# Who adds the last layer's bias: twelve instructions move from VectorE to GpSimd

## The chip, the cores and the metric

The kernel runs on one core of a Trainium2 chip. Its time is the device time of one launch in microseconds (us); the number given is the median of several runs. Before the change it is 401.47 us (three runs, 401.32 to 401.8). The engines are TensorE (PE: matmuls; PEld: its weight loads), VectorE (DVE), ScalarE (ACT), GpSimd (POOL) and SyncE (SP), which issues the DMAs. Each runs its own list of instructions in order; they wait for each other by semaphores. SBUF is the on-chip memory, PSUM the banks into which TensorE writes.

## The reference

`x` is 64 x 128 x 128 (batch, row, feature), `adj` 128 x 128. Cut to what matters:

```python
h = maximum(layernorm(x), 0)
# layer 0: two graph convolutions, then four LSTMs over windows of p rows (p = 1..4)
h = relu(adj @ (h @ Wg0 + bg0));  h = relu(adj @ (h @ Wg1 + bg1))
for p in 1..4:
    windows of p rows of h -> LSTM p (gates i, f, g, o) -> the last hidden
    state replaces the window's last row of h
x = x + h
# layer 1, "the last layer"
h = maximum(layernorm(x), 0)
h0, h1, h2 = h @ W[0], h @ W[1], h @ W[2]
out = diag(adj) * h0 + triu(adj, 1) @ h1 + tril(adj, -1) @ h2 + bias
x = x + out
```

The bias is a vector of 128 features, the same for every batch and row.

## The kernel before

The 64 batches are worked on in four groups of 16 (`GROUPS`, `G`), numbered 0 to 3. A group's layer 0 is 22 LSTM units, k = 0 to 21, in two streams (halves of 8 batches). While group i is in its units, the last layer of group i-1 is woven into them, piece by piece: so the last layers of groups 0, 1 and 2 lie inside the units of groups 1, 2 and 3, called the second, third and fourth pass here. The last layer of group 3 stands alone at the end of the program. A group's 16 batches are four quads (`PACK` = 4 batches, 128 x 512 elements), q = 0 to 3.

What one quad goes through in the last layer, by line:

- The statistics (L1074, L938 to L950 on VectorE) give the negative mean MINUS2 and a variance; GpSimd makes the inverse root of it, RS2 (L387, in `rstd`, a power). 
- Centring: H3 = relu(X - mean). For quads 0 and 1 ScalarE does it, in `centre_up` (L821, semaphore `turned_up`); for quads 2 and 3 VectorE subtracts in `centre` (L1101, semaphore `centred`).
- The bias: X = X + BIAS, `add_bias` (L1117, 128 x 512). It can't come before the centring has read X.
- TensorE transposes H3 (L596); ScalarE and VectorE split the result into two parts, HTH (L799) and HTL (L1108, `turn_down`).
- TensorE multiplies by the three weight matrices, `last_value` (L607 to L609); ScalarE copies the result out of PSUM with RS2 as scale (L812).
- VectorE adds the diagonal term to X, `add_own` (L1129); TensorE makes the two other terms, `last_side` (L615); VectorE adds them to X, `add_out` (L1138), and SyncE stores the quad.

The places of these steps are written out by hand. `START_MID`, `START_BETWEEN` and `START_LATE` say behind which part of which unit VectorE does a step for which quad (`OWN`, `ADD`, `CENTRE`, `SHIFT`, `LOW`; quad -1 is quad 3 of the group before that). `SHIFT` is the bias. `START_LATE` puts it behind unit 5 for quad 0, behind unit 6 for quads 1 and 2, and behind unit 9 for quad 3. In group 3, whose last layer stands alone, GpSimd already adds the bias for quads 0 and 1 (L441), and VectorE for quads 2 and 3. `on_pool` tells who does it, and the stores and `add_own` wait accordingly.

An LSTM unit on VectorE is a chain: the products of gates (L993 where the unit is a window's first step; L996, L1006, L1014 otherwise), then, when ScalarE has made the tanh (L884), the hidden state (L1048), its rounded part (L1052, a cast) and the rest (L1060). TensorE's later units read the last two.

GpSimd's list per group (`group`, L419 to L429) is: the inverse roots for the next group's first layernorm (RS1), and two for this group's RS2. 

Of the kernel before, what the change touches and what calls it, by code (L numbers as in the profile page):

```python
# [8 lines left out]
ALU = mybir.AluOpType  # L9
ACT = mybir.ActivationFunctionType  # L10

B, T, D = 64, 128, 128
G = 16
GROUPS = B // G
# [48 lines left out]
def last_unit(k, s):  # L63
# [23 lines left out]

FILL = {4: 6, 9: 6}

LOW, OWN, ADD, CENTRE, SHIFT = "low", "own", "add", "centre", "shift"  # L90
LAST = QUADS - 1
ON_SCALAR = QUADS // 2

# [12 lines left out]
START_BETWEEN = {0: ((LOW, 0),), 1: ((ADD, -1),), 14: ((ADD, 2),)}  # L106
START_MID = {0: ((OWN, -1),), 4: ((LOW, 1),), 5: ((ADD, 0),), 7: ((OWN, 1),), 8: ((LOW, 2),),
             9: ((ADD, 1),), 12: ((OWN, 2),), 13: ((LOW, 3),)}
START_LATE = {4: ((OWN, 0),), 5: ((CENTRE, 2), (SHIFT, 0)), 6: ((SHIFT, 1), (SHIFT, 2))}
STEADY = Plan(  # L110
    at={**START, (15, 1): (Piece(VALUE, 12, 0, (TURN, 3)),), (16, 3): (Piece(VALUE, 13, 1, (SUM, 2)),),
        (17, 3): (Piece(VALUE, 14, 0, (FORGET, 16)),), (18, 3): (Piece(VALUE, 15, 1, (FORGET, 17)),)},
    f_after={**START_F, 16: (VALUE, 12), 17: (VALUE, 13), 18: (VALUE, 14), 19: (VALUE, 15)},
    quads=QUADS, between=START_BETWEEN, mid=START_MID, late={**START_LATE, 9: ((CENTRE, 3), (SHIFT, 3))})


LATE = Plan(at=START, f_after={**START_F, 16: (TURN, 3), 17: (SUM, 2)}, quads=LAST,
            between=START_BETWEEN, mid=START_MID, late={**START_LATE, 9: ((CENTRE, 3), (SHIFT, 3))})
PLANS = (None,) + (GROUPS - 2) * (STEADY,) + (LATE,)

def on_pool(g, q):

    return g == GROUPS - 1 and q < ON_SCALAR


def shifts_to(g, q):

    return QUADS * g + q + 1 - (ON_SCALAR if g == GROUPS - 1 else 0)  # L130


def present(g, n):
# [27 lines left out]
def program(nc, x_tbd, adj_t, adj_diag, wg0, bg0_col, wg1, bg1, wih_t, whh_t, bih_t, bhh_t, w_l1, bias, out_tbd):  # L161
    with ExitStack() as ctx:
# [171 lines left out]
        @block.sync  # L334
        def _(sp):

            sp.dma_start(X[:, 0:HALF, :], x_tbd[:, 0:HALF, :]).then_inc(x_first, 16)
            for q in range(QUARTERS):
                part = slice(HALF if q == 0 else q * G // QUARTERS, (q + 1) * G // QUARTERS)
                sp.dma_start(X[:, part, :], x_tbd[:, part, :]).then_inc(x_quarter[q], 16)  # L340
                if q == 0:
                    sp.dma_start(ADJ[:, :], adj_t).then_inc(w_adj, 16)
            sp.dma_start(WG0[:, :], wg0).then_inc(w_gcn, 16)
            sp.dma_start(BG0[:, :], bg0_col).then_inc(w_gcn, 16)
            sp.dma_start(WG1[:, :], wg1).then_inc(w_gcn, 16)
            sp.dma_start(BG1[:, :], bg1.rearrange("(a n) -> a n", a=1).broadcast_to([T, D])).then_inc(w_gcn, 16)
            sp.dma_start(BI[:, :], bih_t).then_inc(w_gcn, 16)
            sp.dma_start(BH[:, :], bhh_t).then_inc(w_gcn, 16)
            sp.dma_start(WI[:, :, :], wih_t).then_inc(w_ih, 16)
            sp.dma_start(WH[:, :, :], whh_t).then_inc(w_hh, 16)  # L350
            sp.dma_start(WL1[:, :, :], w_l1).then_inc(w_late, 16)
            sp.dma_start(DIAG[:, :], adj_diag).then_inc(w_late, 16)
            sp.dma_start(BIAS[:, :], bias.rearrange("(a n) -> a n", a=1).broadcast_to([T, D])).then_inc(w_late, 16)
            for g in range(1, GROUPS):
                sp.dma_start(X[:, g * G:(g + 1) * G, :], x_tbd[:, g * G:(g + 1) * G, :]).then_inc(x_rest, 16)


            def store(i):
                for q in range(QUADS):
                    pieces = END_PIECES if i == GROUPS - 1 and q == LAST else ((0, PACK),)  # L360
                    for n, (lo, hi) in enumerate(pieces):
                        if on_pool(i, q):
                            sp.wait_ge(pool_shifted, q + 1)
                        else:
                            sp.wait_ge(shifted_x, shifts_to(i, q))
                        sp.wait_ge(out_ready, QUADS * i + q + 1 + n)
                        part = slice(i * G + q * PACK + lo, i * G + q * PACK + hi)
                        sp.dma_start(out_tbd[:, part, :], X[:, part, :]).then_inc(stored, 16)

            for i in range(GROUPS):  # L370
                store(i)
            sp.wait_ge(stored, 16 * (GROUPS * QUADS + len(END_PIECES) - 1))


        @block.gpsimd
        def _(pool):
            pool.memset(ONES[:, :], 1.0).then_inc(consts, 1)
            pool.memset(NHALF[:, :], -0.5).then_inc(consts, 1)
            pool.memset(IDENT[:, :], 0.0).then_inc(consts, 1)
            pool.wait_ge(consts, 3)  # L380
            pool.affine_select(out=IDENT[:, :], in_=IDENT[:, :], compare_op=ALU.not_equal, fill=1.0,
                               base=0, pattern=[[-1, 128]], channel_multiplier=1).then_inc(consts, 1)

            def rstd(ve, var, count, rs, done, lo, hi):

                pool.wait_ge(var, count)
                pool.tensor_tensor(rs[:, lo:hi], ve[:, lo:hi], NHALF[:, lo:hi], ALU.pow).then_inc(done, 1)  # L387

            pool.wait_ge(consts, 2)
            for q in range(QUARTERS):  # L390
                part = slice(q * G // QUARTERS, (q + 1) * G // QUARTERS)
                rstd(VE1, var1, 2 * q + 2, RS1, rs1, part.start, part.stop)
                pool.wait_ge(rs1, q + 1)
                pool.tensor_tensor(SHIFT1[:, part], MINUS1[:, part], RS1[:, part], ALU.mult).then_inc(shift1, 1)


            pool.wait_ge(consts, 4)
            pool.wait_ge(w_adj, 16)

            for k, sign in enumerate((1, -1)):  # L400
                pool.affine_select(out=ADJ2[:, k, :], in_=ADJ[:, :], compare_op=ALU.is_gt, fill=0.0,
                                   base=0, pattern=[[-sign, T]], channel_multiplier=sign).then_inc(consts, 1)


            pool.wait_ge(w_ih, 16)
            done = 0
            for p in range(POOL_SKIPS):
                pairs = [(WI[:, p, :], WIH[:, p, :], WIL[:, p, :])]
                if p:
                    pool.wait_ge(w_hh, 16)  # L410
                    pairs.append((WH[:, p - 1, :], WHH[:, p - 1, :], WHL[:, p - 1, :]))
                for w, high, low in pairs:
                    pool.tensor_copy(high, w).then_inc(split_w, 1)
                    done += 1
                    pool.wait_ge(split_w, done)
                    pool.tensor_tensor(low, w, high.bitcast(F32), ALU.subtract).then_inc(split_w, 1)
                    done += 1

            def group(i):  # L419
                if i == 0:  # L420
                    for s in range(STREAMS):
                        rstd(VE1, var1, 2 * (QUARTERS + s + 1), RS1, rs1, HB * s, HB * s + HB)
                else:
                    rstd(VE1, var1, 2 * (QUARTERS + i + 2), RS1, rs1, 0, G)
                for s in range(STREAMS):
                    if i > 0:

                        pool.wait_ge(value_sb, G * (i - 1) + HB * (s + 1))
                    rstd(VE2, var2, 2 * STREAMS * i + 2 * s + 2, RS2, rs2, HB * s, HB * s + HB)  # L429

            for i in range(GROUPS - 1):
                group(i)
            i = GROUPS - 1
            for q in range(QUADS):
                pool.wait_ge(value_sb, G * (i - 1) + PACK * (q + 1))
                rstd(VE2, var2, 2 * STREAMS * i + 2 * q + 2, RS2, rs2, PACK * q, PACK * q + PACK)
                if on_pool(i, q):
                    pool.wait_ge(w_late, 48)
                    pool.wait_ge(centred, ON_SCALAR * i + q + 1)
                    part = slice(i * G + q * PACK, i * G + (q + 1) * PACK)  # L440
                    pool.tensor_tensor(X[:, part, :], X[:, part, :],  # L441
                                       BIAS[:, :].unsqueeze(1).broadcast_to([T, PACK, D]),
                                       ALU.add).then_inc(pool_shifted, 1)


        @block.tensor
# [480 lines left out]
        def _(dve):  # L927
# [183 lines left out]

            def add_bias(g, q):

                if q < ON_SCALAR and g < GROUPS - 1:
                    dve.wait_ge(turned_up, ON_SCALAR * g + q + 1)
                part = slice(g * G + q * PACK, g * G + (q + 1) * PACK)
                dve.tensor_tensor(X[:, part, :], X[:, part, :], BIAS[:, :].unsqueeze(1).broadcast_to([T, PACK, D]),  # L1117
                                  ALU.add).then_inc(shifted_x, 1)
# [1 line left out]
            def add_own(g, q, lo=0, hi=PACK):  # L1120

                dve.wait_ge(value_sb, G * g + q * PACK + hi)
                if on_pool(g, q):
                    dve.wait_ge(pool_shifted, q + 1)
                elif g == GROUPS - 1:
                    dve.wait_ge(shifted_x, shifts_to(g, q))
                part = bass.ds(g * G + q * PACK + lo, hi - lo)
                own = as_batches(values(q)[:, 0, :])[:, lo:hi, :]
                dve.scalar_tensor_tensor(out=X[:, part, :], in0=own, scalar=DIAG[:, 0:1],  # L1129
# [47 lines left out]
            def last_step(what, g, q, plan):  # L1177
# [2 lines left out]
                    return  # L1180
                if what == CENTRE:
                    centre(g, q)
                elif what == SHIFT:
                    add_bias(g, q)
                elif what == LOW:
                    turn_down(g, q, home(plan, TURN, q))
                elif what == OWN:
# [137 lines left out]
```

## Time and profile before

| | |
|---|---|
| median of the timed runs | 401.47 us |
| span of the profiled execution, first to last instruction | 399.1 us |
| what the median has beside that span | 2.4 us |
| TensorE matmuls, busy | 393.3 us (99%) |
| VectorE, busy | 346.5 us (87%) |
| ScalarE, busy | 287.4 us (72%) |
| GpSimd, busy | 44.0 us (11%) |
| granted TensorE clock | full in all 40 slices |

The profile is one execution. "Busy" of TensorE counts modelled ends of matmuls that overlap, so small waits of it are seen better in the starts of successive matmuls than in this number. A line of the timeline gives the start and the duration of an instruction (or of a row of equal ones), and in brackets the time that the engine stood still before it, with what ended that.

### The profile page before, as it was taken

Reading aid. Unit: us, or ns where it says so; the run is one execution under the profiler, and the core shown is the slowest. Engines: PE = TensorE matmul, PEld = TensorE weight load, DVE = VectorE, ACT = ScalarE, POOL = GpSimd, SP = SyncE. Lnnn points to the kernel's source line nnn. Section 1 sums busy time; section 2 is a strip of 40 time slices with the busy share of each in tenths; the row PEclk is TensorE's granted clock in tenths of the full one; section 3 lists DMA queues with packets and bytes.
Section 4 is the critical chain, followed back from the end, with each engine's and each line's share of the span. In section 5 each row is a group of like instructions: output and inputs, shape, how many; then the busy total and the mean of one; then the engine's idle time right before and its main releaser. Section 6 shows DMA issues by size and latency. Waiting matters only on the chain.

```text
span 399.1 us, 6598 instructions
## 1 busy us (share of the span) xinstructions
PE 393.3 (99%) x2394; PEld 345.3 (87%) x2394; DVE 346.5 (87%) x886; ACT 287.4 (72%) x579; POOL 44.0 (11%) x44
## 2 busy tenths in 40 slices
PE   8999999999999999999999999999999999999997
PEld 7787889998987789899877879899797788989886
DVE  6569999998998998887998898988898979787897
ACT  4668777875897777777689676777589677767554
POOL 4910200100300003000110000300020000000250
PEclk9999999999999999999999999999999999999999
DMA  7830000000000000000000000000000000000003
GB/s 205 315 140 2 0 0 2 2 0 2 0 1 2 26 28 0 28 2 1 2 16 10 28 0 29 0 28 1 2 2 26 0 28 26 2 26 3 0 0 133
DMA packets 5503, 11.18 MB, mean 28 GB/s; under 512 B 1120, under 2 KB 2528, under 8 KB 4960
## 3 DMA queue, kind: packets, MB, share of 16 engines
q1 hardware_dynamic: 5472, 10.77, 7.5%
q8 instruction: 19, 0.31, 0.4%
q14 instruction: 12, 0.10, 0.1%
HBM read 6.57 MB, written 4.19 MB: 27 GB/s over the span
## 4 chain that ended last, share of the span: by engine, by line
PE 79%; DVE 14%; ACT 4%; issue 1%; DMA 1%; POOL 0%; SPq 0%; DVEq 0%; ACTq 0%
PE PS L549 11%; PE PS L540 11%; PE PS L541 10%; PE PS L572 6%; PE PS L569 6%; PE PS L568 6%; PE PS L615 5%; PE PS L490 4%; PE PS L480 4%; PE PS L472 4%; PE PS L457 3%; PE PS L607 3%; PE PS L608 3%; PE PS L609 3%; ACT GT L869 2%; PE PS L582 1%
## 5 line engine op out<-in xcount | busy, mean ns | idle before, releaser
L869 ACT ACTIVATE GT<-PS,BG 128x256 f32<-128x256 f32 (+2 forms) x312 | 157.9, 563 | 17.5 <-PE PS L572 12.8
L540 PE MATMUL PS<-HH,WIH 128*128 128x256 f32 (+2 forms) x312 | 107.2, 344 | 0.1
L541 PE MATMUL PS<-HH,WIL 128*128 128x256 f32 (+2 forms) x312 | 102.7, 330 | 0.0
L549 PE MATMUL PS<-HL,WIH 128*128 128x256 f32 (+2 forms) x294 | 97.3, 331 | 0.6
L884 ACT ACTIVATE TC<-CS 128x512 f32<-128x512 f32 (+2 forms) x88 | 44.9, 510 | 43.6 <-DVE CS L1014 32.5
L387 POOL TENSOR_TENSOR RS<-VE,NHALF 128x4 f32<-128x4 f32 (+2 forms) x18 | 29.9, 1661 | 344.5 <-DVE VE L950 263.9
L540 PEld LDWEIGHTS PS<-HH,WIH 128*128 128x128 f32 x312 | 58.8, 188 | 9.3 <-DVE HH L1052 4.3
L541 PEld LDWEIGHTS PS<-HH,WIL 128*128 128x128 f32 x312 | 58.9, 189 | 3.9 <-issue 1.2
L549 PEld LDWEIGHTS PS<-HL,WIH 128*128 128x128 f32 x294 | 55.5, 189 | 6.6 <-DVE HL L1060 2.4
L572 PE MATMUL PS<-SL,WHH 128*128 128x256 f32 (+2 forms) x192 | 60.1, 313 | 0.2
L568 PE MATMUL PS<-SH,WHH 128*128 128x256 f32 (+2 forms) x192 | 59.9, 312 | 0.0
L569 PE MATMUL PS<-SH,WHL 128*128 128x256 f32 (+2 forms) x192 | 59.7, 311 | 0.0
L572 PEld LDWEIGHTS PS<-SL,WHH 128*128 128x128 f32 x192 | 36.3, 189 | 2.1 <-DVE SL L1060 0.9
L568 PEld LDWEIGHTS PS<-SH,WHH 128*128 128x128 f32 x192 | 36.2, 189 | 1.5 <-DVE SH L1052 0.2
L996 DVE TENSOR_TENSOR IC<-GT 128x256 f32<-128x256 f32 (+2 forms) x48 | 23.8, 496 | 15.6 <-ACT GT L869 15.4
L569 PEld LDWEIGHTS PS<-SH,WHL 128*128 128x128 f32 x192 | 36.3, 189 | 1.3
L1048 DVE TENSOR_TENSOR HT<-GT,TC 128x256 f32<-128x256 f32 (+2 forms) x48 | 23.8, 495 | 5.8 <-ACT TC L884 4.8
L993 DVE TENSOR_TENSOR CS<-GT 128x512 f32<-128x512 f32 (+2 forms) x40 | 23.9, 597 | 2.6 <-ACT GT L869 2.3
L1060 DVE TENSOR_TENSOR SL<-HT,SH 128x256 fp32r<-128x256 f32 (+2 forms) x48 | 23.9, 497 | 1.5
L812 ACT ACTIVATE WH<-PS,RS 128x384 f32<-128x384 f32 x32 | 17.7, 578 | 10.2 <-PE PS L609 9.6
L1014 DVE TENSOR_TENSOR CS<-IC,CS 128x256 f32<-128x256 f32 (+3 forms) x48 | 23.4, 488 | 1.6
L1048 DVE TENSOR_TENSOR HF<-GT,TC 128x512 f32<-128x512 f32 (+2 forms) x32 | 18.9, 591 | 6.4 <-ACT TC L884 5.7
(95 smaller groups left out, 655.5 us busy)
## 6 DMA issues: line engine op xcount, KB each, us to landing
out_tbd<-X SPq DMA_DIRECT2D x15, 256.0 KB, 2.0
X<-x_tbd SPq DMA_DIRECT2D x3, 1024.0 KB, 12.9
WI<-wih_t SPq DMA_DIRECT2D x1, 1024.0 KB, 5.2
X<-x_tbd SPq DMA_DIRECT2D x3, 256.0 KB, 3.7
WH<-whh_t SPq DMA_DIRECT2D x1, 768.0 KB, 6.6
X<-x_tbd SPq DMA_DIRECT2D x2, 128.0 KB, 2.4
WL<-w_l SPq DMA_DIRECT2D x1, 192.0 KB, 6.4
WG<-wg SPq DMA_DIRECT2D x2, 64.0 KB, 2.8
```

Of the source, the lines that this page charges most:

```text
L387: pool.tensor_tensor(rs[:, lo:hi], ve[:, lo:hi], NHALF[:, lo:hi], ALU.pow).then_inc(done, 1)
L540: pe.matmul(dst, WIH[:, p - 1, cols], x_high, start=True, stop=False)
L541: pe.matmul(dst, WIL[:, p - 1, cols], x_high, start=False, stop=False)
L549: mm = pe.matmul(dst, WIH[:, p - 1, cols], x_low, start=False, stop=(j == 0))
L568: pe.matmul(dst, WHH[:, p - 2, cols], SH[:, s, 0:n], start=False, stop=False)
L569: pe.matmul(dst, WHL[:, p - 2, cols], SH[:, s, 0:n], start=False, stop=False)
L572: pe.matmul(dst, WHH[:, p - 2, cols], SL[:, s, 0:n], start=False, stop=True).then_inc(gate_mm, 1)
L869: act.activation(GT[:, s, q, 0:n], bank(s, q)[:, 0:n], ACT.Tanh if q == C else ACT.Sigmoid, bias=BG[:, 4 * (p - 1) + q:4 * (p - 1) + q + 1 ...
L884: act.activation(TC[:, s, done:n], CS[:, s, done:n], ACT.Tanh).then_inc(tanh_ready, 1)
L993: dve.tensor_tensor(CS[:, s, 0:n], GT[:, s, I, 0:n], GT[:, s, C, 0:n], ALU.mult).then_inc(cell_ready, 1)
L1048: dve.tensor_tensor(full, o, tc, ALU.mult).then_inc(lstm_step, 1)
L1060: dve.tensor_tensor(low, full, high.bitcast(F32), ALU.subtract).then_inc(h_out, 1)
```

## The change

The bias of groups 0, 1 and 2 is added by GpSimd. VectorE's twelve instructions for it (four a group) and the table entries `SHIFT` go. GpSimd gets twelve, at the end of its `group(i)`: behind the second inverse root of RS2, each with a wait on `turned_up` (quads 0, 1) or `centred` (quads 2, 3). `add_own` and the stores wait for GpSimd's semaphore. Group 3 stays as it was: GpSimd for quads 0 and 1, VectorE for 2 and 3.

```diff
-START_LATE = {4: ((OWN, 0),), 5: ((CENTRE, 2), (SHIFT, 0)), 6: ((SHIFT, 1), (SHIFT, 2))}
+START_LATE = {4: ((OWN, 0),), 5: ((CENTRE, 2),), 9: ((CENTRE, 3),)}
...
 def on_pool(g, q):
 
-    return g == GROUPS - 1 and q < ON_SCALAR
+    return g < GROUPS - 1 or q < ON_SCALAR
...
+def pool_shifts_to(g, q):
+
+    return QUADS * g + q + 1
...
+            def add_bias(g, q):
+
+                part = slice(g * G + q * PACK, g * G + (q + 1) * PACK)
+                pool.tensor_tensor(X[:, part, :], X[:, part, :],
+                                   BIAS[:, :].unsqueeze(1).broadcast_to([T, PACK, D]),
+                                   ALU.add).then_inc(pool_shifted, 1)
+
             def group(i):
...
                     rstd(VE2, var2, 2 * STREAMS * i + 2 * s + 2, RS2, rs2, HB * s, HB * s + HB)
+                pool.wait_ge(w_late, 48)
+                for q in range(QUADS):
+                    if q < ON_SCALAR:
+                        pool.wait_ge(turned_up, ON_SCALAR * i + q + 1)
+                    else:
+                        pool.wait_ge(centred, ON_SCALAR * i + q - ON_SCALAR + 1)
+                    add_bias(i, q)
...
@@ VectorE @@
             def add_bias(g, q):
 
-                if q < ON_SCALAR and g < GROUPS - 1:
-                    dve.wait_ge(turned_up, ON_SCALAR * g + q + 1)
                 part = slice(g * G + q * PACK, g * G + (q + 1) * PACK)
...
                 dve.wait_ge(value_sb, G * g + q * PACK + hi)
                 if on_pool(g, q):
-                    dve.wait_ge(pool_shifted, q + 1)
-                elif g == GROUPS - 1:
-                    dve.wait_ge(shifted_x, shifts_to(g, q))
+                    dve.wait_ge(pool_shifted, pool_shifts_to(g, q))
+                else:
+                    dve.wait_ge(shifted_x, shifts_to(q))
```

GpSimd's list where group 0 ends and group 1 begins. RS1 and RS2 are the inverse roots, X the batches. Before:

```order
L387 TENSOR_TENSOR RS1<-VE1,NHALF 128x8 [waits var1] x2
L387 TENSOR_TENSOR RS2<-VE2,NHALF 128x8 [waits var2] x2
L387 TENSOR_TENSOR RS1<-VE1,NHALF 128x16 [waits var1]
L387 TENSOR_TENSOR RS2<-VE2,NHALF 128x8 [waits var2,value_sb] x2
L387 TENSOR_TENSOR RS1<-VE1,NHALF 128x16 [waits var1]
```

And after (`rstd` is on L392, `add_bias` on L427 there):

```order
L392 TENSOR_TENSOR RS1<-VE1,NHALF 128x8 [waits var1] x2
L392 TENSOR_TENSOR RS2<-VE2,NHALF 128x8 [waits var2] x2
L427 TENSOR_TENSOR X<-X,BIAS 128x512 [waits turned_up,w_late]
L427 TENSOR_TENSOR X<-X,BIAS 128x512 [waits turned_up]
L427 TENSOR_TENSOR X<-X,BIAS 128x512 [waits centred] x2
L392 TENSOR_TENSOR RS1<-VE1,NHALF 128x16 [waits var1]
L392 TENSOR_TENSOR RS2<-VE2,NHALF 128x8 [waits var2,value_sb] x2
```

Four adds stand behind a group's second RS2 and in front of the next group's RS1.

VectorE's list in units 5 to 7 of the second pass. H3 is the centred copy; IC and CS are products of gates. Before:

```order
L1101 TENSOR_TENSOR H3<-X,MINUS2 128x512 [waits var2,x_quarter0]
L1117 TENSOR_TENSOR X<-X,BIAS 128x512 [waits turned_up]
L996 TENSOR_TENSOR IC<-GT 128x512 [waits gate_act]
L1006 TENSOR_TENSOR CS<-GT,CS 128x512 [waits gate_act]
L1014 TENSOR_TENSOR CS<-IC,CS 128x512 [waits lstm_step]
L931 BN_STATS ST1<-X 128x6 x4
L1048 TENSOR_TENSOR HF<-GT,TC 128x64x4x2 [waits tanh_ready]
L1052 CAST HH<-HF 128x64x8 [waits lstm_step]
L1060 TENSOR_TENSOR HL<-HF,HH 128x64x8 [waits lstm_step]
L1117 TENSOR_TENSOR X<-X,BIAS 128x512 [waits turned_up]
L1117 TENSOR_TENSOR X<-X,BIAS 128x512
L996 TENSOR_TENSOR IC<-GT 128x512 [waits gate_act]
```

And after:

```order
L1116 TENSOR_TENSOR H3<-X,MINUS2 128x512 [waits var2,x_quarter0]
L1011 TENSOR_TENSOR IC<-GT 128x512 [waits gate_act]
L1021 TENSOR_TENSOR CS<-GT,CS 128x512 [waits gate_act]
L1029 TENSOR_TENSOR CS<-IC,CS 128x512 [waits lstm_step]
L946 BN_STATS ST1<-X 128x6 x4
L1063 TENSOR_TENSOR HF<-GT,TC 128x64x4x2 [waits tanh_ready]
L1067 CAST HH<-HF 128x64x8 [waits lstm_step]
L1075 TENSOR_TENSOR HL<-HF,HH 128x64x8 [waits lstm_step]
L1011 TENSOR_TENSOR IC<-GT 128x512 [waits gate_act]
```

The three adds are gone, and each time the product IC, which waits for ScalarE's gates, comes next. TensorE's and ScalarE's lists are the same before and after.

## Rows read from the trace of the kernel before

**Rows 1.** Page, busy us (share of the span) and instructions, by engine:
```profile
PE 393.3 (99%) x2394; PEld 345.3 (87%) x2394; DVE 346.5 (87%) x886; ACT 287.4 (72%) x579; POOL 44.0 (11%) x44
```
**Rows 2.** Timeline of VectorE, second pass: start us, us, engine, line, instruction, idle before:
```profile
123.53 0.75 DVE L1129 SCALAR_TENSOR_TENSOR X<-WI,DIAG,X 128x512 f32<-128x512 f32 x1
...
128.18 0.69 DVE L1117 TENSOR_TENSOR X<-X,BIAS 128x512 f32<-128x512 f32 x1
129.90 0.69 DVE L996 TENSOR_TENSOR IC<-GT 128x512 f32<-128x512 f32 x1 [1.04 <-ACT GT L869]
...
134.50 1.29 DVE L1117 TENSOR_TENSOR X<-X,BIAS 128x512 f32<-128x512 f32 x2
135.94 0.69 DVE L996 TENSOR_TENSOR IC<-GT 128x512 f32<-128x512 f32 x1 [0.15 <-ACT GT L869]
...
146.87 0.51 DVE L996 TENSOR_TENSOR IC<-GT 128x336 f32<-128x336 f32 x1 [0.27 <-ACT GT L869]
```
**Rows 3.** Timeline of GpSimd, inverse roots of the second and third pass:
```profile
106.61 1.64 POOL L387 TENSOR_TENSOR RS<-VE,NHALF 128x8 f32<-128x8 f32 x1 [4.22 <-DVE VE L950]
154.42 3.09 POOL L387 TENSOR_TENSOR RS<-VE,NHALF 128x16 f32<-128x16 f32 x1 [46.17 <-DVE VE L950]
...
200.63 1.64 POOL L387 TENSOR_TENSOR RS<-VE,NHALF 128x8 f32<-128x8 f32 x1 [5.93 <-DVE VE L950]
```
**Rows 4.** Timeline of GpSimd, at the start and in the last 25 us:
```profile
5.09 1.02 POOL L387 TENSOR_TENSOR RS<-VE,NHALF 128x4 f32<-128x4 f32 x1 [3.38 <-DVE VE L950]
...
376.02 1.52 POOL L387 TENSOR_TENSOR RS<-VE,NHALF 128x4 f32<-128x4 f32 x1 [78.39 <-ACT WH L812]
377.51 1.27 POOL L441 TENSOR_TENSOR X<-X,BIAS 128x512 f32<-128x512 f32 x1
...
381.18 1.55 POOL L441 TENSOR_TENSOR X<-X,BIAS 128x512 f32<-128x512 f32 x1
```
**Rows 5.** Timeline of VectorE beside these last three:
```profile
375.98 0.69 DVE L1101 TENSOR_TENSOR H<-X,MINUS 128x512 f32<-128x512 f32 x1
...
380.84 0.74 DVE L1129 SCALAR_TENSOR_TENSOR X<-WH,DIAG,X 128x512 f32<-128x512 f32 x1
```
**Rows 6.** Timeline of VectorE beside the inverse root at 154.42:
```profile
155.15 0.51 DVE L1060 TENSOR_TENSOR SL<-HT,SH 128x336 fp32r<-128x336 f32 x1
```
**Rows 7.** GpSimd's smallest sum, one line's instructions: ns min/median/max:
```profile
L394 POOL TENSOR_TENSOR SHIFT<-MINUS,RS x4: 199/199/199, 6.2 to 11.2; 128x4 f32<-128x4 f32 x4
```
**Rows 8.** Timeline of VectorE, second pass, units 0 and 1:
```profile
107.87 0.69 DVE L993 TENSOR_TENSOR CS<-GT 128x512 f32<-128x512 f32 x1 [0.15 <-ACT GT L869]
109.26 0.70 DVE L1048 TENSOR_TENSOR HF<-GT,TC 128x512 f32<-128x512 f32 x1 [0.70 <-ACT TC L884]
109.99 0.43 DVE L1052 CAST HH<-HF 128x512 fp32r<-128x512 f32 x1
110.34 0.68 DVE L1108 SCALAR_TENSOR_TENSOR HTL<-PS,HTH 128x512 fp32r<-128x512 f32 x1
```
**Rows 9.** Timeline of TensorE, second pass, the first product of the last layer:
```profile
111.54 0.34 PE L607 MATMUL PS<-WLH,HTH 128*128 128x384 f32 x1
```
**Rows 10.** Timeline of VectorE, third pass, units 0 and 1:
```profile
202.01 0.69 DVE L993 TENSOR_TENSOR CS<-GT 128x512 f32<-128x512 f32 x1 [0.33 <-ACT GT L869]
202.62 0.74 DVE L1129 SCALAR_TENSOR_TENSOR X<-WH,DIAG,X 128x512 f32<-128x512 f32 x1
203.40 0.69 DVE L1048 TENSOR_TENSOR HF<-GT,TC 128x512 f32<-128x512 f32 x1
...
207.54 0.68 DVE L1138 TENSOR_TENSOR X<-PS,X 128x512 f32<-128x512 f32 x1
```
**Rows 11.** Timeline of TensorE, third pass, the product that waits for L1138:
```profile
208.59 0.34 PE L607 MATMUL PS<-WLH,HTH 128*128 128x384 f32 x1
```
**Rows 12.** Timeline of TensorE, second pass, a short stop:
```profile
140.20 0.32 PE L541 MATMUL PS<-HH,WIL 128*128 128x336 f32 x1
140.67 0.42 PE L549 MATMUL PS<-HL,WIH 128*128 128x336 f32 x1
```

More of the change, by code:

```diff
@@ L88 @@
 FILL = {4: 6, 9: 6}
-LOW, OWN, ADD, CENTRE, SHIFT = "low", "own", "add", "centre", "shift"
+LOW, OWN, ADD, CENTRE = "low", "own", "add", "centre"
 LAST = QUADS - 1
@@ L113, with shifts_to @@
     f_after={**START_F, 16: (VALUE, 12), 17: (VALUE, 13), 18: (VALUE, 14), 19: (VALUE, 15)},
-    quads=QUADS, between=START_BETWEEN, mid=START_MID, late={**START_LATE, 9: ((CENTRE, 3), (SHIFT, 3))})
+    quads=QUADS, between=START_BETWEEN, mid=START_MID, late=START_LATE)
 LATE = Plan(at=START, f_after={**START_F, 16: (TURN, 3), 17: (SUM, 2)}, quads=LAST,
-            between=START_BETWEEN, mid=START_MID, late={**START_LATE, 9: ((CENTRE, 3), (SHIFT, 3))})
+            between=START_BETWEEN, mid=START_MID, late=START_LATE)
 PLANS = (None,) + (GROUPS - 2) * (STEADY,) + (LATE,)
 def on_pool(g, q):
-    return g == GROUPS - 1 and q < ON_SCALAR
-def shifts_to(g, q):
-    return QUADS * g + q + 1 - (ON_SCALAR if g == GROUPS - 1 else 0)
+    return g < GROUPS - 1 or q < ON_SCALAR
+def pool_shifts_to(g, q):
+    return QUADS * g + q + 1
+def shifts_to(q):
+    return q + 1 - ON_SCALAR
 def present(g, n):
@@ L362, in store @@
                         if on_pool(i, q):
-                            sp.wait_ge(pool_shifted, q + 1)
+                            sp.wait_ge(pool_shifted, pool_shifts_to(i, q))
                         else:
-                            sp.wait_ge(shifted_x, shifts_to(i, q))
+                            sp.wait_ge(shifted_x, shifts_to(q))
                         sp.wait_ge(out_ready, QUADS * i + q + 1 + n)
@@ L437, in _ @@
                 if on_pool(i, q):
-                    pool.wait_ge(w_late, 48)
                     pool.wait_ge(centred, ON_SCALAR * i + q + 1)
[L440 to L443, printed above, removed]
+                    add_bias(i, q)
         @block.tensor
@@ L1182, in last_step @@
                     centre(g, q)
-                elif what == SHIFT:
-                    add_bias(g, q)
                 elif what == LOW:
```

## The prediction

> **What bounds the kernel now.** I began with the busy times on the page: TensorE 99%, VectorE 87%, GpSimd 11% [rows 1]. So what matters is not how much VectorE does but whether it makes TensorE stop. The second view was the timeline of VectorE at the bias adds that go. The reader is to see the bracket behind each: after the first add the next instruction, IC on L996, comes after 1.04 us of idleness, after the pair at 134.50 after 0.15 us, and after the add in front of 146.87 after 0.27 us, each time ended by ScalarE's gate (L869), which in turn waits for TensorE [rows 2]. The third and fourth pass show the same instructions with about the same spacing. The third view was GpSimd's timeline, for when the new adds can run [rows 3] and for what happens when both engines are at work [rows 4, 5, 6]. The last was VectorE and TensorE side by side where the new adds will fall [rows 8 to 11].
>
> **What goes.** Four adds a group, twelve in all, at 0.60 to 0.69 us each (a pair takes 1.29) [rows 2]: some 8 us of VectorE's time. Each stood in a gap that ScalarE's gates ended, so VectorE only waits longer: 1.04 + 0.6 us at the first place, 0.15 + 1.2 at the second, 0.27 + 0.6 at the third. Gain: 0. The edits of waits cost nothing: `add_own` for quad 0 comes at 123.53 [rows 2], some 12 us after GpSimd can be done with it (below), and the other quads have more room. The stores wait for `out_ready`, which comes later than the bias in either kernel.
>
> **What comes, and when.** GpSimd's adds stand behind the second RS2 of a group. This ends at 106.61 + 1.64 = 108.25 in the second pass and at 200.63 + 1.64 = 202.27 in the third [rows 3]; the fourth repeats the third. ScalarE's centring is over by then, so the adds for quads 0 and 1 start at once, one after the other. The add for quad 2 follows the centring that ends about where the old add began, 128.2, and ends near 129.5, inside the gap before 129.90 [rows 2]: it meets nothing. The one for quad 3 runs from about 146.0 to 147.2 and meets IC at 146.87 [rows 2], 0.3 to 0.5 us of delay. TensorE has a whole unit of the other stream to do before it reads what comes of this IC, so I cost it at 0; without that cover it would be 3 x 0.45 = 1.4 us. GpSimd's next inverse root comes at 154.42 [rows 3], 7 us later.
>
> How long is such an add? Alone 1.27 us (at 377.51) [rows 4], twice the time of VectorE's. The one at 381.18 took 1.55. What differs is the company: at 380.84 VectorE had begun L1129, which reads two operands from SBUF, and it lets go about 0.65 us later, at 381.5, 0.3 after GpSimd's start [rows 5]. The inverse roots tell the same: 128x4 takes 1.02 at the start, but 1.52 at 376.02, where VectorE had begun the two-operand L1101 at 375.98 [rows 4, 5]. So there is one thing both need to read SBUF with, and GpSimd waits until VectorE's instruction is through. Whether VectorE waits for GpSimd likewise, no row shows for an add: in the rows the VectorE instructions beside the long GpSimd ones read PSUM or one operand. Beside the inverse root at 154.42 VectorE's two-operand L1060 starts and runs as ever, 0.51 [rows 6], but that GpSimd instruction reads 16 columns and then computes for 3 us; an add reads 1,024 columns.
>
> So the price has two ends. Low end: VectorE never waits, 0. High end: VectorE waits for the whole 1.27 us of an add whenever it wants two operands. The value I take: the thing is held for the add's time less the fixed part of a small GpSimd sum, 0.20 [rows 7], so 1.07 us. Rows 4 and 5 are the nearest, and they show exclusion, not sharing.
>
> The Trainium skill, page "SBUF — State Buffer", section "Who interferes with whom", says that a VectorE instruction with two SBUF inputs contends with a GpSimd instruction that reads SBUF, and that whoever comes second blocks for the whole instruction. The rows agree for one direction (1.52 against 1.02); no row shows the other. By that rule the high end would hold.
>
> **Second pass** [rows 8, 9]. Successive VectorE instructions start 0.60 us apart. L993 of 107.87 lets go at 108.48; the first add holds until 109.55. L1048, due at 109.26, starts at 109.55 and lets go at 110.15. The second add, ready at 109.75, holds from 110.15 to 111.22. The cast L1052, due 0.73 behind L1048, starts at 111.22 instead of 109.99 if a cast is shut out too (it has one operand, but runs at 0.43 where others take 0.69, so I suppose that it reads with both ports; if not, this pass costs nothing). HTL (L1108) comes 0.35 later, at 111.57, and is done at 112.25 instead of 111.02. TensorE needs it at 111.54: 112.25 - 111.54 = 0.71 us of stop.
>
> **Third pass** [rows 10, 11]. L993 of 202.01 lets go at 202.61; the first add holds to 203.68. L1129, due at 202.62, starts at 203.68 and lets go at 204.35. The second add holds to 205.42. L1048, due at 203.40, starts at 205.42: 2.02 late. What follows is a chain of its own results and tanhs, so the lateness stays, and L1138 starts at 209.56 and ends at 210.24. TensorE's L607 of 208.59 waits for it: 210.24 - 208.59 = 1.65 us. The fourth pass repeats the third: 1.65 again.
>
> Sum: 0.71 + 2 x 1.65 = 4.0 us on a span of 399.1. With the 2.4 us that the median of 401.47 has beside this span: 405.5 us. TensorE is at work nearly all the time, so what it loses isn't given back later. With 1.27 for the hold the same steps give 1.11 + 2 x 2.05 = 5.2, so 406.7; with casts not shut out, 404.8.
>
> **Rivals.**
> 1. VectorE doesn't wait, or only for moments: an add reads in small pieces between which VectorE gets its turn. For it: rows 6. Against it: GpSimd waits out VectorE's whole instruction [rows 4, 5], and an add reads nearly all its time. The adds then cost nothing, since GpSimd has 12 us of room, and nothing is gained: 401.5.
> 2. Faster: behind the pair of adds VectorE has only 0.15 us left [rows 2]. If IC in truth waited for the adds (gates done earlier than their record says), the chain from IC over the tanh to the hidden state comes earlier, and TensorE's stop at 140.67 shrinks: its starts are 0.47 apart there [rows 12]. Three passes: at most 1.4 us, likelier 0.9, so 400.6, and it decides only if the adds of units 0 and 1 cost under that. Against it: the bracket names ScalarE in the second pass.
> 3. GpSimd comes too late: if VectorE's instructions always win and the adds starve, `add_own` waits, or the next RS1 at 154.42. For quads 0 and 1 this needs 12 us of starving, and rows 4 show an add that waited 0.3. It would be 407 or more.
>
> **Numbers.** The forecast's case (VectorE shut out, 402.3 to 406.8 by the length of the hold and what a cast does) has 0.57; rival 1 has 0.33; rival 2 has 0.08; rival 3 has 0.02. The measurement tells a change from none at 0.2%, or 0.8 us. A part of the first case could still end under that, and a part of the first rival above it, about equal. So faster 0.08, same 0.34, slower 0.58. The likeliest case gives 405.5, its own range 402.3 to 406.8; the range that is to hold the time 8 times in 10 must take in rival 1: 401.0 to 406.8.
>
> **What would show it.** Right: in the windows from 108.2 to 111.3 and from 202.3 to 205.5 GpSimd shows two adds, and between VectorE's L993 and HTL of that place stand gaps or longer instructions that ScalarE doesn't end, about 1.2 us in the second pass and 2 in the third; TensorE's L607 at 208.59 comes over 1 us late, and the span grows by as much as those stops together. VectorE's busy time falls by some 8 us without any use. Wrong: the adds at 108.3 and 202.3 take 1.5 us and more each while VectorE's starts keep their spacing; then it is rival 1. If the span falls and the stop at 140.67 with it, it is rival 2. The forecast is also wrong in its size if VectorE, coming back to back, keeps GpSimd waiting until a natural gap, since then only one add is in its way.

## The result, and the profile after

| | before | changed |
|---|---|---|
| median of the timed runs | 401.41 us (4 runs, 401.32 to 401.8) | 406.23 us (4 runs, 405.99 to 406.58) |
| ratio, with its 95% interval | | 1.0121 (1.0107 to 1.0136) |
| span of the profiled execution | 399.1 us | 404.4 us |
| VectorE busy | 346.5 us | 345.5 us |
| GpSimd busy | 44.0 us | 61.2 us |

The kernel became 4.8 us slower. In the changed kernel's numbering the lines are: L392 the inverse root (L387 before), L427 GpSimd's bias add, L1008 (L993), L1011 (L996), L1063 (L1048), L1067 (L1052), L1123 (L1108), L1142 (L1129), L1151 (L1138), L622 (L607).

The page of the changed kernel, busy times:

```profile
PE 395.2 (98%) x2394; PEld 345.9 (86%) x2394; DVE 345.5 (85%) x874; ACT 287.3 (71%) x579; POOL 61.2 (15%) x56
```

Twelve instructions of some 0.6 to 0.69 us have left VectorE, yet its busy time fell by 1.0 us only: three of those that stayed take longer in each pass, by 6.65 us in all. The timelines show which. GpSimd of the changed kernel, second and third pass (start us, us, instruction, idle before), against [rows 3]:

```profile
106.51 1.64 POOL L392 TENSOR_TENSOR RS<-VE,NHALF 128x8 f32<-128x8 f32 x1 [4.22 <-DVE VE L965]
108.11 3.24 POOL L427 TENSOR_TENSOR X<-X,BIAS 128x512 f32<-128x512 f32 x2
129.56 1.31 POOL L427 TENSOR_TENSOR X<-X,BIAS 128x512 f32<-128x512 f32 x1 [18.21 <-DVE H L1116]
...
202.25 1.64 POOL L392 TENSOR_TENSOR RS<-VE,NHALF 128x8 f32<-128x8 f32 x1 [5.92 <-DVE VE L965]
203.85 3.33 POOL L427 TENSOR_TENSOR X<-X,BIAS 128x512 f32<-128x512 f32 x2
```

VectorE beside them, second pass, against [rows 8]:

```profile
107.77 0.69 DVE L1008 TENSOR_TENSOR CS<-GT 128x512 f32<-128x512 f32 x1 [0.15 <-ACT GT L884]
109.16 1.01 DVE L1063 TENSOR_TENSOR HF<-GT,TC 128x512 f32<-128x512 f32 x1 [0.70 <-ACT TC L899]
110.21 1.43 DVE L1067 CAST HH<-HF 128x512 fp32r<-128x512 f32 x1
111.56 0.68 DVE L1123 SCALAR_TENSOR_TENSOR HTL<-PS,HTH 128x512 fp32r<-128x512 f32 x1
```

And third pass, against [rows 10]:

```profile
203.63 0.69 DVE L1008 TENSOR_TENSOR CS<-GT 128x512 f32<-128x512 f32 x1 [0.34 <-ACT GT L884]
204.24 1.81 DVE L1142 SCALAR_TENSOR_TENSOR X<-WH,DIAG,X 128x512 f32<-128x512 f32 x1
205.97 1.76 DVE L1063 TENSOR_TENSOR HF<-GT,TC 128x512 f32<-128x512 f32 x1
...
211.17 0.68 DVE L1151 TENSOR_TENSOR X<-PS,X 128x512 f32<-128x512 f32 x1
```

A wait for the other engine shows as length of the waiting instruction and not as idle time: L1142 takes 1.81 us instead of 0.74, L1063 1.76 instead of 0.69, the cast 1.43 instead of 0.43. HTL, which reads PSUM and one SBUF operand, has its 0.68 as before. TensorE waits for what comes out of this. First the chain of waits in the second pass, merged (start us, us, what; "issue" is time in which nothing that the trace shows was waited for), then TensorE's timeline in the third pass, against [rows 9, 11]:

```profile
109.16 1.02 DVE HF L1063
110.19 0.02 issue
110.21 1.43 DVE HH L1067
111.64 0.61 DVE HTL L1123
112.25 0.14 issue
112.38 0.42 PE PS L622
```

```profile
210.01 0.40 PE L564 MATMUL PS<-HL,WIH 128*128 128x512 f32 x1
211.91 0.45 PE L622 MATMUL PS<-WLH,HTH 128*128 128x384 f32 x1 [1.50 <-DVE X L1151]
```

TensorE has the same 2,394 matmuls in the same order in both traces, so the lateness of each can be read by taking the start of the n-th from that of the n-th. Up to the second pass the changed kernel's trace stands 0.10 us ahead; at the end it is 5.24 us behind. The lateness grows at these places and hardly anywhere else (places by the time in the trace of before): 0.94 us at 111.5, 0.37 more until 117.0, 0.36 at 190.5, 1.67 at 208.6 and 0.11 right behind, 1.66 at 304.0 and 0.11 right behind. That is 5.2 us of the 5.3 by which the span grew (404.4 - 399.1).

What went brought nothing. IC in units 6 and 7 now waits longer for ScalarE, against [rows 2]:

```profile
131.11 0.69 DVE L1011 TENSOR_TENSOR IC<-GT 128x512 f32<-128x512 f32 x1 [1.63 <-ACT GT L884]
...
137.15 0.69 DVE L1011 TENSOR_TENSOR IC<-GT 128x512 f32<-128x512 f32 x1 [1.36 <-ACT GT L884]
```

### The profile page after: what moved, and what is told of

It is laid out like the page before. It is cut to its first block, busy times and chain, and to the rows that moved or that the text cites. A ratio compares the mean times of both kernels' runs of the same rounds, so it can differ in the third digit from the quotient of the medians.

```text
span 404.4 us, 6611 instructions
## 1 busy us (share of the span) xinstructions
PE 395.2 (98%) x2394; PEld 345.9 (86%) x2394; DVE 345.5 (85%) x874; ACT 287.3 (71%) x579; POOL 61.2 (15%) x56
## 4 chain that ended last, share of the span: by engine, by line
PE 71%; DVE 21%; ACT 6%; issue 2%; POOL 0%; DVEq 0%; ACTq 0%; POOLq 0%
PE PS L564 9%; PE PS L555 9%; PE PS L556 9%; PE PS L587 5%; PE PS L584 5%; PE PS L583 5%; PE PS L630 4%; ACT GT L884 4%; PE PS L505 4%; PE PS L495 4%; PE PS L487 3%; PE PS L622 3%; PE PS L623 3%; PE PS L472 3%; PE PS L624 2%; DVE HF L1063 2%
## 5 line engine op out<-in xcount | busy, mean ns | idle before, releaser
L392 POOL TENSOR_TENSOR RS<-VE,NHALF 128x4 f32<-128x4 f32 (+2 forms) x18 | 29.6, 1644 | 225.1 <-DVE VE L965 186.8
L1011 DVE TENSOR_TENSOR IC<-GT 128x256 f32<-128x256 f32 (+2 forms) x48 | 24.9, 519 | 21.9 <-ACT GT L884 21.8
L427 POOL TENSOR_TENSOR X<-X,BIAS 128x512 f32<-128x512 f32 x14 | 20.5, 1473 | 107.4 <-DVE H L1116 107.4
L1063 DVE TENSOR_TENSOR HT<-GT,TC 128x256 f32<-128x256 f32 (+2 forms) x48 | 23.8, 495 | 5.9 <-ACT TC L899 5.0
L622 PE MATMUL PS<-WLH,HTH 128*128 128x384 f32 x64 | 22.7, 355 | 4.1 <-DVE X L1151 3.0
L1063 DVE TENSOR_TENSOR HF<-GT,TC 128x512 f32<-128x512 f32 (+2 forms) x32 | 21.4, 669 | 6.1 <-ACT TC L899 5.4
L1008 DVE TENSOR_TENSOR CS<-GT 128x512 f32<-128x512 f32 (+2 forms) x40 | 23.9, 596 | 2.6 <-ACT GT L884 2.3
```

The source lines that it names most:

```text
L622: pe.matmul(dst, high, w_high, start=True, stop=False)
L1011: dve.tensor_tensor(IC[:, s, 0:n], GT[:, s, I, 0:n], GT[:, s, C, 0:n], ALU.mult).then_inc(lstm_step, 1)
L1063: dve.tensor_tensor(full, o, tc, ALU.mult).then_inc(lstm_step, 1)
```

## The experiments

The theory: while a GpSimd add reads SBUF, VectorE's instructions with two SBUF operands (and its casts) wait for it whole, and that alone costs. The rivals: GpSimd's adds cost wherever they are; the new semaphore waits cost; any work of GpSimd does. Each run stands beside runs of the kernel before of the same set; its median was 401.41 us beside the changed kernel, and 401.29, 401.36 and 401.37 us in the three sets of the others. In the table "idle" means that nobody waits for the instruction or reads what it writes.

| kernel | median us | ratio to before, 95% interval |
|---|---|---|
| changed kernel | 406.23 | 1.0121 (1.0107 to 1.0136) |
| adds of quads 0, 1 ahead of the second root | 401.46 | 1.0003 (0.9994 to 1.0012) |
| quads 2, 3 alone on GpSimd | 401.38 | 1.0002 (0.9993 to 1.0011) |
| quads 0, 1 alone on GpSimd | 405.86 | 1.0114 (1.0100 to 1.0128) |
| before + idle adds, one repeated tile | 404.40 | 1.0075 (1.0059 to 1.0090) |
| before + idle adds, two full tiles | 405.96 | 1.0115 (1.0100 to 1.0130) |
| before + idle copies | 402.07 | 1.0018 (1.0008 to 1.0027) |
| before + memsets | 401.08 | 0.9994 (0.9985 to 1.0003) |
| changed, adds in halves | 404.56 | 1.0080 (1.0064 to 1.0097) |
| quads 0, 1 alone, ahead of the second root | 401.08 | 0.9992 (0.9983 to 1.0001) |
| all on GpSimd, also in the last stage | 401.50 | 1.0003 (0.9995 to 1.0012) |

**The same adds, 6 us earlier.** Against the changed kernel:

```diff
                     rstd(VE2, var2, 2 * STREAMS * i + 2 * s + 2, RS2, rs2, HB * s, HB * s + HB)
-                pool.wait_ge(w_late, 48)
-                for q in range(QUADS):
...
+                    if s == 0:
+                        pool.wait_ge(w_late, 48)
+                        for q in range(ON_SCALAR):
+                            pool.wait_ge(turned_up, ON_SCALAR * i + q + 1)
+                            add_bias(i, q)
+                for q in range(ON_SCALAR, QUADS):
+                    pool.wait_ge(centred, ON_SCALAR * i + q - ON_SCALAR + 1)
                     add_bias(i, q)
```

> The changed kernel, with GpSimd's adds for quads 0 and 1 placed ahead of the second inverse root of RS2 instead of behind it. By the trace of before they then run at about 102.4 to 105 us in the second pass and 196.3 to 199 in the third, where VectorE's instructions read PSUM or a single SBUF operand. Theory (VectorE's two-operand and cast instructions wait for a GpSimd add as a whole, and only this costs): 401.4 us, within 0.2% of the kernel before; L1063 and the cast in units 0 and 1 are back at 0.69 and 0.43 us. Rival (GpSimd's adds cost wherever they stand, by load on SBUF or by the new waits of add_own and the stores): 404 to 406.5.

Measured: 401.46 us, no change from before. GpSimd's timeline, then VectorE's beside it and in unit 0, second pass (here L427 is the add; L987 and L996 read PSUM and one SBUF operand, L1090 is the statistics with one operand, L1064 and L1068 are hidden state and cast):

```profile
100.87 1.64 POOL L392 TENSOR_TENSOR RS<-VE,NHALF 128x8 f32<-128x8 f32 x1 [24.69 <-DVE VE L966]
102.47 2.50 POOL L427 TENSOR_TENSOR X<-X,BIAS 128x512 f32<-128x512 f32 x2
```

```profile
100.70 2.48 DVE L987 TENSOR_TENSOR Y<-PS,BG 128x512 f32<-128x512 f32 x4
103.09 1.64 DVE L1090 BATCH_NORM_STATS2 ST<-X 128x6 f32<-128x128 f32 x8
104.65 1.27 DVE L996 SCALAR_TENSOR_TENSOR HL<-PS,HH 128x512 fp32r<-128x512 f32 x2
...
109.37 0.69 DVE L1064 TENSOR_TENSOR HF<-GT,TC 128x512 f32<-128x512 f32 x1 [0.70 <-ACT TC L900]
110.10 0.45 DVE L1068 CAST HH<-HF 128x512 fp32r<-128x512 f32 x1
```

The pair takes 2.50 us instead of 3.24, and the VectorE instructions beside it have the durations that they have in the kernel before (2.48, 1.64 and 1.28 us there). All twelve adds are on GpSimd here, with all the new waits, and they cost nothing. So it is the place, not their number or the semaphores.

**Which quads.** Two kernels that split the change: GpSimd adds for quads 2 and 3 and VectorE for 0 and 1 at its old places, and the other way round. The line of `on_pool` that differs in the first (in the second it has 0 and 1; the entries `SHIFT` of the quads that VectorE keeps are back in `START_LATE`):

```diff
-    return g < GROUPS - 1 or q < ON_SCALAR
+    return q in (2, 3) if g < GROUPS - 1 else q < ON_SCALAR
```

> Undoes the change for quads 0 and 1 alone: VectorE adds their bias at its old places, GpSimd adds that of quads 2 and 3 behind the centring. Theory: the six adds of quads 0 and 1 carry the whole loss, so 401.4 us (at most 0.5 above it, from IC in unit 10, which the add of quad 3 delays by 0.2 to 0.4 us a pass off TensorE's path). Rival (loss in proportion to the number of GpSimd's adds): 403.8.

> The counterpart: GpSimd adds the bias of quads 0 and 1 alone (behind the second root), VectorE that of quads 2 and 3. Theory: the whole loss stays, 405.7 to 406.3 us. Rival (proportion): 403.8.

Measured: 401.38 and 405.86 us. The six adds of quads 0 and 1 carry the loss, those of quads 2 and 3 none. In the first of the two, IC in unit 10 does wait for the add of quad 3 (0.87 us against 0.51 in [rows 2]), and no matmul comes later for it. VectorE's timeline of that kernel:

```profile
146.82 0.87 DVE L1011 TENSOR_TENSOR IC<-GT 128x336 f32<-128x336 f32 x1 [0.87 <-ACT GT L884]
```

**Adds that touch nothing of the kernel.** To the kernel before, behind the second root of each group, writing into a new tile SCR:

```diff
+                for n in range(2):
+                    ones = ONES[:, :].unsqueeze(1).broadcast_to([T, PACK, D])
+                    pool.tensor_tensor(as_batches(SCR[:, n, :]), ones, ones, ALU.add)
```

> The kernel before, unchanged but for two GpSimd instructions a group behind the second inverse root: sums of ONES with ONES (128x512, two operands) into a scratch tile that nobody reads and nobody waits for. So no semaphore, no wait and no tile of the kernel is touched. Theory (what GpSimd reads with is held): as the changed kernel, 405.5 to 406.5 us, with L1048 and L1052 of unit 0 stretched to about 1.0 and 1.4 us in the second pass. Rival (the new semaphore waits, or both engines at work on X): 401.4.

Measured: 404.40 us. The rival is out: nobody waits for these adds and they share no tile with VectorE's work. But the size missed the expectation of 405.5 to 406.5. VectorE's timeline, third pass (L1133 is the diagonal term, L1052 the hidden state here), then GpSimd's:

```profile
203.55 1.53 DVE L1133 SCALAR_TENSOR_TENSOR X<-WH,DIAG,X 128x512 f32<-128x512 f32 x1
205.00 1.53 DVE L1052 TENSOR_TENSOR HF<-GT,TC 128x512 f32<-128x512 f32 x1
```

```profile
203.15 2.83 POOL L433 TENSOR_TENSOR SCR<-ONES 128x512 f32<-128x512 f32 x2
```

The hold, the time by which a VectorE instruction gets longer, is 1.53 - 0.74 = 0.79 and 1.53 - 0.69 = 0.84 us, not 1.07. The next kernel has two full tiles as operands:

```diff
-                    ones = ONES[:, :].unsqueeze(1).broadcast_to([T, PACK, D])
-                    pool.tensor_tensor(as_batches(SCR[:, n, :]), ones, ones, ALU.add)
+                    pool.tensor_tensor(SCR[:, n, :], WIL[:, 0, :].bitcast(F32), WIH[:, 0, :].bitcast(F32), ALU.add)
```

> As the idle sums in the kernel before, but of two different, full 128x512 tiles of split weights, where the first form read one 128x128 tile repeated, for both operands. That form held VectorE for 0.79 us an add (L1129 1.53 against 0.74), the changed kernel's add for 1.07. Theory A (the hold is the reading, and reading a repeated tile is shorter): 1.07 here, 405.9 us. Theory B (writing back to the tile that is read, as the bias add does on X, makes the difference): 0.8 here, 404.4.

Measured: 405.96 us, the whole loss, with VectorE's timeline of the third pass (L1132, L1051), then GpSimd's:

```profile
204.38 1.78 DVE L1132 SCALAR_TENSOR_TENSOR X<-WH,DIAG,X 128x512 f32<-128x512 f32 x1
206.09 1.76 DVE L1051 TENSOR_TENSOR HF<-GT,TC 128x512 f32<-128x512 f32 x1
```

```profile
204.00 3.30 POOL L432 TENSOR_TENSOR SCR<-WIL,WIH 128x512 f32<-128x512 f32 x2
```

The holds are 1.04 and 1.07 us although nothing is written back to what is read, so theory B is out and theory A stands. The two GpSimd lines say more: the pair on one repeated tile takes 2.83 us, the pair on full tiles 3.30 at the same place, some 0.24 an add, which is about what the hold is shorter by. So the add on one repeated tile is itself a shorter instruction. What shortens it (the repetition, or that both operands are the same) was not separated; the bias add repeats BIAS alone and holds 1.07.

**Less reading.** Copies (one operand) and memsets (none) in the same place of the kernel before, first the copies:

```diff
+                for n in range(2):
+                    pool.tensor_copy(as_batches(SCR[:, n, :]), ONES[:, :].unsqueeze(1).broadcast_to([T, PACK, D]))
```

and the memsets:

```diff
+                for n in range(4):
+                    pool.memset(SCR[:, n, :], 1.0)
```

> The kernel before, with two GpSimd copies (128x512, one operand) a group in place of the idle sums. Theory (held while GpSimd reads; a copy takes 0.61 us, less 0.2 fixed gives a hold of 0.4): L1129 and L1048 in the third pass 0.3 to 0.4 us longer each, TensorE's stop 0.4 us a pass in the third and fourth and none in the second: 402.2 us. Rival (only a GpSimd instruction with two operands shuts VectorE out): 401.3.

> The kernel before, with four GpSimd memsets (128x512 each, write only) a group behind the second inverse root, into scratch that nobody reads: GpSimd is busy from about 108.3 us on as in the changed kernel, but reads nothing from SBUF. Theory (VectorE's second operand and GpSimd's reads go through one thing): two-operand instructions keep 0.69 us, time 401.3 us; the cast of unit 0 may be longer if a cast also writes through it, at most 0.2 us on the time. Rival (GpSimd at work beside VectorE is enough, whatever it does): 404 to 406.

Measured: 402.07 and 401.08 us. VectorE's timeline with the copies, third pass (L1132, L1051), then GpSimd's and VectorE's with the memsets, same place:

```profile
203.14 1.10 DVE L1132 SCALAR_TENSOR_TENSOR X<-WH,DIAG,X 128x512 f32<-128x512 f32 x1
204.16 1.10 DVE L1051 TENSOR_TENSOR HF<-GT,TC 128x512 f32<-128x512 f32 x1
```

```profile
202.34 1.93 POOL L432 MEMSET SCR<- 128x512 f32 x4
```

```profile
202.75 0.75 DVE L1132 SCALAR_TENSOR_TENSOR X<-WH,DIAG,X 128x512 f32<-128x512 f32 x1
203.53 0.69 DVE L1051 TENSOR_TENSOR HF<-GT,TC 128x512 f32<-128x512 f32 x1
```

A copy holds for 0.36 and 0.41 us, the memsets not at all, though they are at work through both instructions. So two operands on GpSimd's side are not needed, and reading is. Of the cast the memsets tell next to nothing: in the second pass they ended at 110.23, and the cast had begun at 110.09.

**Cut in halves.** Against the changed kernel, each add as two of 128x256 (and the counts of the semaphore doubled):

```diff
+                for lo in range(0, PACK, HALF):
+                    part = slice(g * G + q * PACK + lo, g * G + q * PACK + lo + HALF)
...
+                                       BIAS[:, :].unsqueeze(1).broadcast_to([T, HALF, D]),
```

> The changed kernel with each GpSimd add cut into two of 128x256. The whole reading stays, but VectorE gets a turn between the halves. Theory (held per instruction, some 0.53 us a half): lateness at L1138 in the third pass 1.4 us instead of 2.0, TensorE's stops 0.5 + 1.1 + 1.1 instead of 0.93 + 1.68 + 1.65, time 404.7 us; VectorE's instructions there 0.4 to 0.55 longer, each. Rival (what counts is the whole of what GpSimd reads while VectorE wants to): 406.2.

Measured: 404.56 us; TensorE's lateness grows by 0.51, 0.97 and 0.98 us at its three stops. VectorE's timeline, third pass (L1143, L1064, L1068, L1124):

```profile
204.05 1.23 DVE L1143 SCALAR_TENSOR_TENSOR X<-WH,DIAG,X 128x512 f32<-128x512 f32 x1
205.20 1.23 DVE L1064 TENSOR_TENSOR HF<-GT,TC 128x512 f32<-128x512 f32 x1
206.46 0.83 DVE L1068 CAST HH<-HF 128x512 fp32r<-128x512 f32 x1
207.21 0.68 DVE L1124 SCALAR_TENSOR_TENSOR HTL<-PS,HTH 128x512 fp32r<-128x512 f32 x1
```

Three instructions wait 0.49, 0.54 and 0.40 us, each for one half, and the fourth half falls beside HTL, which isn't held. So the engines take turns by instructions here, and the smaller ones lose less, since some of their reading meets nothing.

**Two tries at a better version.**

> GpSimd adds the bias of quads 0 and 1 alone, ahead of the second root; VectorE keeps quads 2 and 3. By the theory nothing meets: as before. What it tells apart: a stop of TensorE of 0.45 us in front of L472 at 190.7 us showed in the changed kernel, in the one with all adds moved ahead of the root and in the one with quads 2 and 3 on GpSimd, and not in the one with quads 0 and 1 on GpSimd, whose VectorE list is the same as here. If the stop comes from VectorE's list it is absent here, and the time is 401.2 us; if it comes from when GpSimd's adds end, it is here, and the time is 401.7.

> The adds ahead of the second root for groups 0 to 2, and in group 3 all four quads on GpSimd, so that VectorE adds no bias at all: its two adds at 390.9 and 394.2 us of the last stage go. A try at a version that beats both. Theory: TensorE leads that stage (the chain that ended last is TensorE's from 380 to 396.5 us), so at most 0.3 us are gained, against 0.45 for the stop at 190.7: 401.0 to 401.7 us, no change from before. Rival (VectorE sets the last stage's end): 400.2, 1.2 us gained.

The first is the early placing with VectorE keeping quads 2 and 3; the second the early placing with `on_pool` always true and VectorE's two adds of group 3 taken out (the early placing isn't shown again):

```diff
-    return g < GROUPS - 1 or q < ON_SCALAR
+    return True
...
-            add_bias(i, 2)
...
-            add_bias(i, LAST)
```

Measured: 401.08 and 401.50 us, neither told apart from the kernel before. So no version found here beats it. The second shows the same trap in the last stage. VectorE's timeline there (L1152 reads PSUM, L1143 is the diagonal term), and GpSimd's:

```profile
389.41 1.28 DVE L1152 TENSOR_TENSOR X<-PS,X 128x512 f32<-128x512 f32 x2
390.61 1.56 DVE L1143 SCALAR_TENSOR_TENSOR X<-WH,DIAG,X 128x512 f32<-128x512 f32 x1
```

```profile
390.35 1.27 POOL L427 TENSOR_TENSOR X<-X,BIAS 128x512 f32<-128x512 f32 x1
```

The last add began 0.26 us ahead of L1143, while VectorE was reading PSUM, and made it 0.82 longer: the 0.6 of the add taken from VectorE came back as waiting, and TensorE's lateness grows by 0.22 us at 392.4.

## Why the prediction was right, point by point

- **What goes brings nothing**: right. ScalarE's gates still end the waits of IC (1.63 and 1.36 us of idleness now), and TensorE's starts gained nothing there.
- **When the new adds run**: right. The pair starts at 108.11 and 203.85, right behind the roots; quad 2's add (129.56 to 130.87) meets nothing; quad 3's makes IC 0.36 us longer (0.87 against 0.51), and the split kernel shows that this costs nothing.
- **VectorE waits for GpSimd too**: this was the step that the trace of before didn't show, and which held 0.57 of the chance. It is right: 1.81 against 0.74 us in the changed kernel, 0.75 with memsets in the same place.
- **How the wait would show**: half right. "Gaps or longer instructions" was forecast, together with a VectorE busy time some 8 us lower. Only the second form came, and it takes that fall back: busy fell by 1.0 us, since 6.65 us of waiting now count as busy.
- **The hold, 1.07 us**: measured 1.07 and 1.07 in the third pass, 1.04 and 1.07 in the fourth. It was GpSimd's 1.27 less the 0.20 of its smallest sum, a choice between two ends and no more, and it came out. The high end, the whole 1.27, and with it the rule that the prediction cites for it, was 0.20 too much.
- **A cast waits too**: right wherever an add met a cast (1.43 us with whole adds, 0.83 with halves, against 0.43). It was a supposition from the cast's short time.
- **Second pass, 0.71 us**: TensorE's stop was 0.94. The term lacked the 0.14 us between the end of HTL and the start of the matmul, which the chain shows as issue. The other 0.09 is hidden by a coincidence: HTL starts at 111.56, forecast 111.57, but the changed kernel's trace stands 0.10 us ahead at this place (107.77 against 107.87), so the delay on VectorE was 0.09 longer than forecast.
- **Third and fourth pass, 1.65 us each**: 1.67 and 1.66. L1151 came 211.17 - 207.54 = 3.63 us later than in before, 1.62 of that being what the pass was late already (203.63 - 202.01): 2.01, forecast 2.02.
- **The sum, 4.0 us**: 5.3 in the trace. Beside the 0.23 of the second pass it lacked 0.59 of small stops behind the large ones (VectorE stays late by more than TensorE has waited: 0.37, 0.11 and 0.11) and 0.36 at 190.5 (last section); the rest comes in bits of 0.06 and less. The time itself was missed by only 0.7, 405.5 against 406.23, and that is in part luck: the sum was 1.3 too small, but what the time has beside the span was taken as 2.4 and is 1.8 here (406.23 - 404.4). The low end of the range of this case, 402.3, isn't worked out in the prediction; no run comes near enough to test it.
- **The rivals**: sharing in small pieces is out, since in every kernel in which a reading GpSimd instruction met a two-operand one of VectorE, the VectorE instruction was held until that one was nearly through. The faster one is out too: the time rose, and no stop of TensorE shrank. GpSimd never came too late.

## What to carry to other kernels

Before moving elementwise work to GpSimd, look what VectorE does at the moment at which it will run. Beside instructions that read PSUM or a single SBUF operand it was free here (401.46 us for all twelve adds). Beside two-operand sums and casts an add held VectorE for 1.0 to 1.07 us where it met one in full, more than the 0.6 that it had saved. Such waiting shows as a longer instruction, not as idle time, so compare durations of the same instruction. And take the price only where the waiting engine leads: quad 3's add held VectorE too, and cost nothing.

## What the runs showed of the hardware that was not expected

- Among GpSimd instructions that read as they go, the hold follows their own time: 1.04 to 1.07 us for a 128x512 add of 1.27 us; 0.40 to 0.54 for a 128x256 add of 0.74; 0.36 to 0.41 for a copy of 0.61; 0.79 to 0.84 for the add of one repeated tile with itself, which is some 0.24 shorter than other adds. Each is within 0.15 us of the instruction's time less 0.2 (by the trace, whose times for GpSimd are rough). Being busy alone isn't enough: four memsets in 1.93 us held nobody, nor did an inverse root of 3.09 us in the rows of before [rows 3, 6].
- In the changed kernel, those with the early adds of all quads (alone and with the last stage), the one with quads 2 and 3 on GpSimd, and the one in halves, the matmul at 190.5 starts 0.86 to 0.88 us after the one ahead of it, and in all others 0.49 to 0.52. It stands behind VectorE's statistics, which start 0.45 us late with nothing to wait for that the trace names. The changed kernel's timeline of VectorE:

```profile
188.06 1.28 DVE L1082 TENSOR_TENSOR X<-PS,X 128x512 f32<-128x512 f32 x2
189.79 1.65 DVE L1089 BATCH_NORM_STATS2 ST<-X 128x6 f32<-128x128 f32 x8 [0.45 <-DVE X L1082]
```

The kernels without the stop are those that keep before's list on VectorE, and the two that took only quads 0 and 1 from it. The last of them to run was to tell whether VectorE's list or the end of GpSimd's adds decides, and the stop was absent, as expected for the list. But the kernels with the stop are also just those in which GpSimd adds the bias of quads 2 and 3, so the two aren't separated. In the kernels with the stop an 8 KB load of instructions that the others have at 180.0 to 181.8 us comes at 189.2 to 190.6. It comes 0.67 us or more after the statistics have begun, that is, after VectorE's stop is over, so its landing isn't what VectorE waited for; the cause of the stop stays open. The stop is a part of the changed kernel's trace, but not of its verdict: the kernel with the early adds has it and is no slower than before beyond the measurement.
